# Reordering the first stage of a fused language-model tower: squares before tables, a weight's centring on ScalarE, rows worked ahead in two engines

## The chip, the cores and the metric

The kernel runs on one core of one Trainium2 chip. The metric is the device time of one execution in microseconds (us). The engines are named as the profile names them: PE is TensorE (PEld its weight loads), DVE is VectorE, ACT is ScalarE, POOL is GpSimd, SP is SyncE, which here only issues DMAs.

## The reference

The model takes 32 sequences of 128 tokens, with a vocabulary of 28, and has three parts. Cut to what matters here:

```python
h = tok(x, mask)                              # embedding + windowed features, fused @ fus_w, LayerNorm
h = h + attn(layernorm(h), Wq, Wk, Wv, Wo)    # 16 heads of 64, softmax, then LayerNorm(x + ctx @ Wo)
h = h + moe(layernorm(h))                     # 16 experts of 64, top 2, top 64 tokens of each expert
```

Before attention every token is a combination of 56 table rows (28 one-hot columns and 28 averages over neighbours), plus two constant rows. So each token's first LayerNorm needs only a quadratic form of its 56 coefficients, and the query, key, value and output weights can be multiplied with the 64-row table once, instead of with 4096 tokens. The last LayerNorm of attention subtracts a mean over 256 features; the kernel takes that mean out of the rows of Wo beforehand ("centring of the output weight").

## The kernel before

It is one program in three blocks, and at the end of each block all engines meet before the next one starts. The first block (lines 212 to 638) makes the tables; the second (751 to 1214) runs attention over 32 sequences; the third (1283 to 1538) runs the experts. Only the first block is touched. Each engine runs its own instruction list strictly in the order written, with semaphore waits between them; nobody plans or reorders. The core of the first block, after the table of 64 rows (`mt`) is there, is:

- **quads(g)**, for four octets g of sequences. PE L580 multiplies the transposed coefficients `nT` with a Gram matrix `cs` held in three bf16 parts (24 matmuls in two banks, `QUAD_BANKS[g % 2]`); DVE L423 multiplies the result with the coefficients `nb` (two instructions), and DVE L427 sums it into `red`. PE may refill a pair of banks only when DVE has read them (`prod_ok`).
- **roots**, DVE L445 to L455 with two square roots on ACT (L300): `r1`, `r2`, `r12`, `sig` for all 32 sequences, in a chain of small instructions. After the second root ACT loads the table for Exp (L301).
- **u_rows(g)**: DVE L460 and L461 scale the coefficients into `uf`; ACT L305 rounds them to f16 (`uh`, named u_hi); DVE L463 takes the remainder (`ul`).
- **u_cols(g)**: PE L597 transposes `uh` and `ul` of an octet into four banks, `UT_BANKS` (16 matmuls); ACT L309 copies each bank to `ub`. For the next octet PE waits for the copies of the one before, bank by bank (`ut_ok`).
- **table(n)**, n = 0, 1, 2 for Wq, Wk, Wv: PE L566 makes 16 fp32 products with `mt` (32 instructions in the trace), DVE L413 copies the bank to `qkv_t`, DVE L415 adds the bias column. Table 2 uses the bank of table 0 and waits for its copy.
- **centre_wo**: DVE L481, L483, L485 sum the rows of Wo (`wo_v`, 128x8x256), scale the sums and add them back in place.
- **gram**: PE L605 multiplies tables 0 and 1 head by head; ACT L314 (g_hi) and then DVE L468 (g_lo) store it as two f16 parts `gp`.
- **z_part(n)**, four of them: PE L619 multiplies table 2 with Wo in fp32; ACT L320 (z_hi) and then DVE L475 (z_lo) store it as `zh` and `zl`.
- **keep_going(n)**: n matmuls (L506) whose result nobody reads.

The lists of the three engines from there on, before the change: PE table(0), quads(0) to (3) with eight fillers ahead of (2) and of (3), table(1), table(2), eight fillers, u_cols(0), gram, then eight fillers and u_cols(g) for g = 1, 2, 3, and z_part(0) to (3). DVE centre_wo, table(0), four quads, roots, u_rows(0), table(1), u_rows(1), table(2), g_lo, u_rows(2), u_rows(3), four z_lo; each u_rows there has the remainder L463 in it. ACT stands in lines 298 to 337. POOL splits the expert weight w1 meanwhile (L268 to L272). SP issues its loads early, ahead of all this, in an order that isn't touched; Wo is the last of the four large weights (L235).

Of the kernel before, what the change touches and what calls it, by code (L numbers as in the profile page):

```python
# [89 lines left out]
def build(nc, d, out):  # L90
    with ExitStack() as ctx:
# [40 lines left out]
        def sb1(name, shape, dt=F32):  # L132
            return sb(name, shape, dt, one)
# [26 lines left out]
        wsum = sb1("wsum", [P, 2, HD])  # L160
# [22 lines left out]
        uf_ok, uh_ok, ul_ok, ut_ready, ut_ok = (sem(n) for n in ("uf_ok", "uh_ok", "ul_ok", "ut_ready", "ut_ok"))  # L183
# [28 lines left out]
        with nc.Block() as block:  # L212
# [66 lines left out]
            def _(act):  # L279
# [18 lines left out]
                for n, (v, root) in enumerate(((v1, q1), (v2, q2))):  # L298
                    act.wait_ge(v_ok, n + 1)
                    nc.scalar.activation(root[:], v[:], ACT.Sqrt).then_inc(sqrt_ok, 1)  # L300
                nc.scalar.preload_act_table(ACT.Exp)  # L301

# [22 lines left out]
                for n in range(4):  # L325
                    u_cols(0, n)
                g_hi()
                u_hi(2)
                for n in range(4):
                    u_cols(1, n)  # L330
                u_hi(3)
                for n in range(4):
                    u_cols(2, n)
                for n in range(4):
                    u_cols(3, n)
                for n in range(4):
                    z_hi(n)

            @block.vector
            def _(dve):  # L340
# [69 lines left out]
                def table(n):  # L410
                    dve.wait_ge(in_w[n], 32)
                    dve.wait_ge(qkv_ready, n + 1)
                    nc.vector.tensor_copy(qkv_t[:, n], TABLE_BANKS[n][:].rearrange("p (c u) -> p c u", c=HD)).then_inc(qkv_ok, 1)  # L413
                    dve.wait_ge(qkv_ok, 2 * n + 1)
                    nc.vector.tensor_copy(qkv_t[:, n, :, ONE:ONE + 1], bT[:, n, :].rearrange("p (c o) -> p c o", o=1))\  # L415
                        .then_inc(qkv_ok, 1)

# [38 lines left out]

                def u_rows(g):
# [3 lines left out]
                    nc.vector.tensor_copy(uf[:, s, R2:R2 + 1], r2[:, s].rearrange("p (b o) -> p b o", o=1)).then_inc(uf_ok, 1)  # L461
                    dve.wait_ge(uh_ok, g + 1)
# [16 lines left out]
                def centre_wo():  # L479
                    dve.wait_ge(in_wo, 16)  # L480
                    nc.vector.reduce_sum(wsum[:, 0, :], wo_v, AX.X).then_inc(wo_step, 1)  # L481
                    dve.wait_ge(wo_step, 1)
                    nc.vector.tensor_scalar(wsum[:, 1, :], wsum[:, 0, :], -1.0 / D, None, ALU.mult).then_inc(wo_step, 1)  # L483
                    dve.wait_ge(wo_step, 2)
                    nc.vector.tensor_tensor(wo_v, wo_v, bcast(wsum[:, 1, :], D), ALU.add).then_inc(wo_step, 1)  # L485

                centre_wo()
                table(0)
# [4 lines left out]
                table(1)  # L493
                u_rows(1)
                table(2)
                g_lo()
                u_rows(2)
                u_rows(3)
# [4 lines left out]
            def _(pe):  # L503
# [81 lines left out]
                def u_cols(g):  # L585
# [5 lines left out]
                    for n in range(4):  # L591
                        if g >= 1:
                            pe.wait_ge(ut_ok, 4 * g - 3 + n)
# [16 lines left out]
                def z_part(n):  # L610
                    if n == 0:
                        pe.wait_ge(wo_step, 3)
                        pe.wait_ge(qkv_ok, 6)
                        pe.wait_ge(glo_ok, len(G_PARTS))
# [8 lines left out]

                table(0)
                for g in range(NQ):
                    if g >= 2:
                        keep_going(8, psum[0][:, 0:FREE])
                    quads(g)
# [5 lines left out]
                for g in range(1, NQ):  # L634
                    keep_going(8, psum[5][:, 0:FREE])
                    u_cols(g)
# [958 lines left out]
```

## Time and profile before

| | |
|---|---|
| median of 3 runs | 570.81 us (569.54 to 571.08) |
| the profiled execution | 572.44 us, of which the span from first to last instruction is 570.7 us |
| first block | 0 to 66.8 us of the span |
| busy PE, DVE, ACT, POOL over the whole span | 526.0, 453.3, 357.1, 387.5 us |
| mean granted clock of PE | 0.963 of full speed |

How to read it: the page's busy shares are means over three blocks. PE is 92% busy over the whole span, which is set by the two later blocks. What matters here is the first block, and in it which engine each other engine waits for. The strip of the whole span in 40 slices of 14.3 us shows it: PE is granted its full clock nearly everywhere except in slices 3 to 5.

```
PE   4797788999999999999999999839999999999985
DVE  5785466889888888888888888977846888887776
ACT  1215767788787877878878787614784655565540
PEclk9957799999999999999999999987999999999998
```

### The profile page before, as it was taken

What the parts mean: (1) busy time and instruction counts of PE and PEld (TensorE: products, weight loads), DVE (VectorE), ACT (ScalarE), POOL (GpSimd) and SP (SyncE); (2) the same over time, 40 slices, a digit from 0 to 9 for tenths busy, and PEclk for the clock granted to TensorE, in tenths of its full rate; (3) what the DMA queues carried; (4) which work ended last, traced back from release to release, by engine and by line L of the source; (5) the groups of instructions that cost most, each with busy time, mean ns of one, the idle gap of its engine ahead of it and who ended that gap; (6) DMA issues with size and microseconds to landing.
All of it is one profiled execution on the core that took longest, in us unless ns stands there. A gap on an engine that the chain in (4) does not pass through costs nothing. (4 is left out here: it accounts for less than half of the span.)

```text
span 570.7 us, 16170 instructions
## 1 busy us (share of the span) xinstructions
PE 526.0 (92%) x6063; PEld 395.0 (69%) x6063; DVE 453.3 (79%) x1019; ACT 357.1 (63%) x744; POOL 387.5 (68%) x512
## 2 busy tenths in 40 slices
PE   4797788999999999999999999839999999999985
PEld 2697666778777777777777777624457777777774
DVE  5785466889888888888888888977846888887776
ACT  1215767788787877878778787614584655565540
POOL 3050235888787877878778787942095977898783
PEclk9957799999999999999999999987999999999998
DMA  6800000000000000000000000000633044053011
GB/s 208 325 2 1 2 1 2 4 3 2 3 3 3 2 3 3 3 3 3 4 3 2 4 3 3 2 0 2 151 85 83 20 110 102 22 141 85 24 45 55
DMA packets 11905, 21.73 MB, mean 38 GB/s; under 512 B 4668, under 2 KB 9780, under 8 KB 10164
## 3 DMA queue, kind: packets, MB, share of 16 engines
q1 hardware_dynamic: 11828, 20.71, 13.1%
q8 instruction: 48, 0.79, 0.6%
q14 instruction: 29, 0.24, 0.1%
HBM read 16.24 MB, written 4.33 MB: 36 GB/s over the span
## 5 line engine op out<-in xcount | busy, mean ns | idle before, releaser
L768 POOL TENSOR_TENSOR s_pl<-s_pf,s_ph 128x512 f16<-128x512 f32 x128 | 147.0, 1160 | 15.3 <-ACT s_ph L860 15.3
L949 DVE TENSOR_REDUCE s_mx<-ps 128x4 f32<-128x512 f32 x128 | 83.8, 677 | 29.1 <-PE ps L1090 29.1
L1503 PE MATMUL ps<-s_xt_all,s_w1s 128*128 128x512 f16 x384 | 89.9, 387 | 0.8 <-PEq L751 0.8
L1526 PE MATMUL ps<-s_w2s,s_hid 128*128 128x256 f16 x768 | 88.9, 273 | 0.0
L854 ACT ACTIVATE s_pf<-ps 128x512 f32<-128x512 f32 x128 | 76.6, 602 | 16.9 <-PE ps L1103 16.9
L1526 PEld LDWEIGHTS ps<-s_w2s,s_hid 128*128 128x128 f16 x768 | 75.1, 98 | 11.1
L860 ACT ACTIVATE s_ph<-s_pf 128x512 f16<-128x512 f32 x128 | 77.2, 637 | 0.0
L1136 PE MATMUL ps<-s_zh,s_cth 128*128 128x256 f16 x256 | 69.8, 273 | 0.0
L1136 PE MATMUL ps<-s_zl,s_cth 128*128 128x256 f16 x256 | 69.8, 273 | 0.0
L1136 PE MATMUL ps<-s_zh,s_ctl 128*128 128x256 f16 x256 | 69.8, 273 | 0.0
L1503 PEld LDWEIGHTS ps<-s_xt_all,s_w1s 128*128 128x128 f16 x384 | 38.1, 100 | 42.4 <-issue 4.5
L1120 PE MATMUL ps<-s_uh,s_ph 128*128 128x64 f16 x512 | 51.5, 193 | 0.4 <-issue 0.4
L1120 PE MATMUL ps<-s_ul,s_ph 128*128 128x64 f16 x512 | 51.5, 193 | 0.0
L1120 PE MATMUL ps<-s_uh,s_pl 128*128 128x64 f16 x512 | 51.5, 193 | 0.0
L1341 POOL TENSOR_TENSOR s_hid<-s_ub,s_hid 128x512 f16<-128x512 f32 x24 | 29.8, 1264 | 29.3 <-ACT s_hid L1382 29.1
L1103 PE MATMUL ps<-s_qh,s_ub 64*128 64x512 f16 x256 | 48.9, 379 | 0.0
L847 ACT ACTIVATE s_qh<-ps 128x512 f16<-128x512 f32 x64 | 38.1, 596 | 16.3 <-PE ps L1103 14.3
L940 DVE SCALAR_TENSOR_TENSOR s_ql<-ps,s_qh 128x512 f16<-128x512 f32 x64 | 43.3, 678 | 5.2 <-ACT s_qh L847 5.2
L1120 PEld LDWEIGHTS ps<-s_uh,s_ph 128*128 128x128 f16 x512 | 46.1, 98 | 1.1 <-issue 0.6
L1120 PEld LDWEIGHTS ps<-s_ul,s_ph 128*128 128x128 f16 x512 | 45.4, 98 | 0.7
L1120 PEld LDWEIGHTS ps<-s_uh,s_pl 128*128 128x128 f16 x512 | 45.5, 98 | 0.0
L970 DVE TENSOR_TENSOR s_ctl<-ps,s_cth 128x512 f16<-128x512 f32 x64 | 43.6, 682 | 0.4 <-ACT s_cth L866 0.3
(230 smaller groups left out, 1252.3 us busy)
## 6 DMA issues: line engine op xcount, KB each, us to landing
s_rep<-picks SPq DMA_DIRECT2D x14, 512.0 KB, 6.6
s_stage<-in_w SPq DMA_DIRECT2D x2, 1024.0 KB, 13.9
out<-s_ot_a SPq DMA_DIRECT2D x16, 128.0 KB, 1.7
out<-s_lg SPq DMA_DIRECT2D x16, 128.0 KB, 1.7
s_stage<-in_wq SPq DMA_DIRECT2D x1, 1024.0 KB, 4.7
s_stage<-in_wk SPq DMA_DIRECT2D x1, 1024.0 KB, 6.4
s_stage<-in_wv SPq DMA_DIRECT2D x1, 1024.0 KB, 8.1
s_stage<-in_wo SPq DMA_DIRECT2D x1, 1024.0 KB, 9.9
```

The lines of the kernel that those rows point to most:

```text
L768: nc.gpsimd.tensor_tensor(flat(pl[:, b % 2, 4 * j:4 * j + 4, :]), pf[:, j, :], flat(ph[:, b % 2, 4 * j:4 * j + 4, :]), ALU.subtract).then_ ...
L847: nc.scalar.activation(flat(qh[:, b % 2, hf]), A[hf][:], ACT.Copy, scale=1.0 / G_SCALE)\
L854: nc.scalar.activation(pf[:, j, :], ST[j % 2][:], ACT.Exp).then_inc(exp_done[j], 1)
L860: nc.scalar.activation(flat(ph[:, b % 2, 4 * j:4 * j + 4, :]), pf[:, j, :], ACT.Copy).then_inc(phi_done[j], 1)
L940: nc.vector.scalar_tensor_tensor(out=flat(ql[:, b % 2, hf]), in0=A[hf][:], scalar=1.0 / G_SCALE, in1=flat(qh[:, b % 2, hf]), op0=ALU.mult, ...
L949: nc.vector.tensor_reduce(mx[:, b % 2, c:c + 4], A[ab][:].rearrange("p (h k) -> p h k", h=4), AX.X, ALU.max).then_inc(max_done[hf][ab], 1)
L970: nc.vector.tensor_tensor(flat(ctl[:, b % 2, 4 * hf:4 * hf + 4, :]), CB[hf][:], flat(cth[:, b % 2, 4 * hf:4 * hf + 4, :]), ALU.subtract).t ...
L1103: mm = nc.tensor.matmul(ST[ab][:], ub[r, b, part, :], flat(q[r, b % 2, hf]), start=(n == 0), stop=(n == 2))
L1120: mm = nc.tensor.matmul(CB[hf][:, c:c + UD], p[:, b % 2, h, :], u[:, b, 0, :], start=(n == 0), stop=(n == 2))
L1136: nc.tensor.matmul(YB[:, 0:D], c[:, b % 2, p, :], zz[:, p, :], start=(p == 0 and c is cth and zz is zh), stop=False)
L1503: mm = nc.tensor.matmul(HB[j % NH][:], w1s[:, wp, c, j * P:(j + 1) * P], xt_all[:, GB * g:GB * (g + 1), xp, c, :], start=(k == 0), stop=(k ...
L1526: mm = nc.tensor.matmul(zb[b % 4], hid[:, g % 2, hp, j, t * P:(t + 1) * P], w2s[:, wp, j, :], start=False, stop=(j == NJ - 1 and hp == 1))
```

## The change

Within the first block, with no work added to or taken from the result:

- PE issues twelve fillers, quads(0), quads(1), then table(0), then quads(2), quads(3), table(1), table(2). The fillers ahead of quads(2) and (3) are gone; those ahead of the later u_cols are six instead of eight.
- Centring of the output weight moves from DVE (three instructions) to ACT: eight sums of 256 columns by an Identity with an accumulator, each waiting for the one before, one scaling, and eight in-place additions (Identity with a bias per partition).
- The copies of the three tables and of their bias columns move from DVE to ACT, placed between the centring steps and the square roots.
- DVE starts with the quads. Its u_rows is split in scaling (`u_rows`) and remainder (`u_lo`), and scaling is issued one octet ahead. ACT's u_hi(2) comes ahead of the copies of octet 0, and u_hi(3) ahead of g_hi.
- The fourth bank of each octet's u_cols is copied by DVE instead of ACT, with a semaphore of its own (`ut_last_ok`). ACT's copies of octet 3 go between z_hi(1) and z_hi(2).

```diff
--- before.py
+++ after.py
@@ -157,7 +157,7 @@
         mt = sb1("mt", [P, 2, KC, 2, UD])
         cs, cres = sb1("cs", [P, 3, P], BF16), sb1("cres", [P, P])
         s_eps = sb1("s_eps", [P, 1])
-        wsum = sb1("wsum", [P, 2, HD])
+        wsum, wo_sum = sb1("wsum", [P, 2, HD]), sb1("wo_sum", [P, D])
         prod = tok[:, 0:B // 2, :].rearrange("p n (k a u) -> p (n k) a u", k=2, a=2)
         red = sb1("red", [P, B, 2])
         v1, r1, t1, q1, t2, t3, v2, r2, r12, q2 = (
@@ -180,7 +180,7 @@
         quad_ready, prod_ok, red_ok = sem("quad_ready"), sem("prod_ok"), sem("red_ok")
         root_step, v_ok, sqrt_ok = sem("root_step"), sem("v_ok"), sem("sqrt_ok")
         root_count = [0]
-        uf_ok, uh_ok, ul_ok, ut_ready, ut_ok = (sem(n) for n in ("uf_ok", "uh_ok", "ul_ok", "ut_ready", "ut_ok"))
+        uf_ok, uh_ok, ul_ok, ut_ready, ut_ok, ut_last_ok = (sem(n) for n in ("uf_ok", "uh_ok", "ul_ok", "ut_ready", "ut_ok", "ut_last_ok"))
         qkv_ready, qkv_ok, g_ready, ghi_ok, glo_ok, z_ready, zhi_ok, zlo_ok, wo_step = (
             sem(n) for n in ("qkv_ready", "qkv_ok", "g_ready", "ghi_ok", "glo_ok", "z_ready", "zhi_ok", "zlo_ok", "wo_step"))
 
@@ -295,10 +295,32 @@
                 nc.scalar.activation(tts[0:UD, :], tm[:], ACT.Copy, scale=T_SCALE).then_inc(tts_ok, 1)
                 nc.scalar.activation(mr[0:UD, :], mbo[:], ACT.Copy, scale=Y_SCALE).then_inc(mr_ok, 1)
 
-                for n, (v, root) in enumerate(((v1, q1), (v2, q2))):
+                def root(n, v, r):
                     act.wait_ge(v_ok, n + 1)
-                    nc.scalar.activation(root[:], v[:], ACT.Sqrt).then_inc(sqrt_ok, 1)
+                    nc.scalar.activation(r[:], v[:], ACT.Sqrt).then_inc(sqrt_ok, 1)
+
+                def table(n):
+                    act.wait_ge(in_w[n], 32)
+                    act.wait_ge(qkv_ready, n + 1)
+                    nc.scalar.activation(qkv_t[:, n], TABLE_BANKS[n][:].rearrange("p (c u) -> p c u", c=HD), ACT.Copy).then_inc(qkv_ok, 1)
+                    act.wait_ge(qkv_ok, 2 * n + 1)
+                    nc.scalar.activation(qkv_t[:, n, :, ONE:ONE + 1], bT[:, n, :].rearrange("p (c o) -> p c o", o=1), ACT.Copy)\
+                        .then_inc(qkv_ok, 1)
+
+                act.wait_ge(in_wo, 16)
+                for c in range(HD):
+                    nc.scalar.activation(wo_sum[:], wo_v[:, c, :], ACT.Identity, accum_out=wsum[:, 0, c:c + 1]).then_inc(wo_step, 1)
+                    act.wait_ge(wo_step, c + 1)
+                nc.scalar.activation(wsum[:, 1, :], wsum[:, 0, :], ACT.Copy, scale=-1.0 / D).then_inc(wo_step, 1)
+                act.wait_ge(wo_step, HD + 1)
+                table(0)
+                for c in range(HD):
+                    nc.scalar.activation(wo_v[:, c, :], wo_v[:, c, :], ACT.Identity, bias=wsum[:, 1, c:c + 1]).then_inc(wo_step, 1)
+                root(0, v1, q1)
+                table(1)
+                root(1, v2, q2)
                 nc.scalar.preload_act_table(ACT.Exp)
+                table(2)
 
                 def u_hi(g):
                     act.wait_ge(uf_ok, 2 * g + 2)
@@ -322,19 +344,20 @@
 
                 u_hi(0)
                 u_hi(1)
-                for n in range(4):
+                u_hi(2)
+                for n in range(3):
                     u_cols(0, n)
+                u_hi(3)
                 g_hi()
-                u_hi(2)
-                for n in range(4):
-                    u_cols(1, n)
-                u_hi(3)
-                for n in range(4):
-                    u_cols(2, n)
-                for n in range(4):
+                for g in (1, 2):
+                    for n in range(3):
+                        u_cols(g, n)
+                z_hi(0)
+                z_hi(1)
+                for n in range(3):
                     u_cols(3, n)
-                for n in range(4):
-                    z_hi(n)
+                z_hi(2)
+                z_hi(3)
 
             @block.vector
             def _(dve):
@@ -407,14 +430,6 @@
                 nc.vector.scalar_tensor_tensor(out=mr[UD:P, :], in0=mbo[:], scalar=Y_SCALE, in1=mr[0:UD, :],
                                                op0=ALU.mult, op1=ALU.subtract).then_inc(mr_ok, 1)
 
-                def table(n):
-                    dve.wait_ge(in_w[n], 32)
-                    dve.wait_ge(qkv_ready, n + 1)
-                    nc.vector.tensor_copy(qkv_t[:, n], TABLE_BANKS[n][:].rearrange("p (c u) -> p c u", c=HD)).then_inc(qkv_ok, 1)
-                    dve.wait_ge(qkv_ok, 2 * n + 1)
-                    nc.vector.tensor_copy(qkv_t[:, n, :, ONE:ONE + 1], bT[:, n, :].rearrange("p (c o) -> p c o", o=1))\
-                        .then_inc(qkv_ok, 1)
-
                 def quads(g):
                     for par in range(2):
                         dve.wait_ge(quad_ready, 2 * g + par + 1)
@@ -454,11 +469,19 @@
                     then(nc.vector.tensor_tensor(r12[:], r1[:], r2[:], ALU.mult))
                     then(nc.vector.scalar_tensor_tensor(out=sig[:], in0=v2[:], scalar=1.0 / T_SCALE, in1=r2[:], op0=ALU.mult, op1=ALU.mult))
 
+                def u_cols(g):
+                    dve.wait_ge(ut_ready, 4 * g + 4)
+                    nc.vector.tensor_copy(ub_b[:, 4 * g + 3, :], UT_BANKS[3][:]).then_inc(ut_last_ok, 1)
+
                 def u_rows(g):
                     s = octet(g)
                     dve.wait_ge(cleared, CLEARED["uf"])
                     nc.vector.tensor_tensor(uf[:, s, 0:2 * V], nb[:, s, 0:2 * V], bcast(r12[:, s], 2 * V), ALU.mult).then_inc(uf_ok, 1)
                     nc.vector.tensor_copy(uf[:, s, R2:R2 + 1], r2[:, s].rearrange("p (b o) -> p b o", o=1)).then_inc(uf_ok, 1)
+
+                def u_lo(g):
+                    s = octet(g)
+                    dve.wait_ge(uf_ok, 2 * g + 2)
                     dve.wait_ge(uh_ok, g + 1)
                     nc.vector.tensor_tensor(ul[:, s], twice(uf[:, s, :]), uh[:, s], ALU.subtract).then_inc(ul_ok, 1)
 
@@ -476,26 +499,21 @@
                                                    scalar=Y_SCALE, in1=zh[:, zc, :], op0=ALU.mult, op1=ALU.subtract)\
                         .then_inc(zlo_ok, 1)
 
-                def centre_wo():
-                    dve.wait_ge(in_wo, 16)
-                    nc.vector.reduce_sum(wsum[:, 0, :], wo_v, AX.X).then_inc(wo_step, 1)
-                    dve.wait_ge(wo_step, 1)
-                    nc.vector.tensor_scalar(wsum[:, 1, :], wsum[:, 0, :], -1.0 / D, None, ALU.mult).then_inc(wo_step, 1)
-                    dve.wait_ge(wo_step, 2)
-                    nc.vector.tensor_tensor(wo_v, wo_v, bcast(wsum[:, 1, :], D), ALU.add).then_inc(wo_step, 1)
-
-                centre_wo()
-                table(0)
                 for g in range(NQ):
                     quads(g)
                 roots()
                 u_rows(0)
-                table(1)
                 u_rows(1)
-                table(2)
+                u_lo(0)
+                u_rows(2)
+                u_lo(1)
+                u_cols(0)
+                u_rows(3)
+                u_lo(2)
                 g_lo()
-                u_rows(2)
-                u_rows(3)
+                u_lo(3)
+                for g in range(1, NQ):
+                    u_cols(g)
                 for n in range(4):
                     z_lo(n)
 
@@ -589,8 +607,10 @@
                     if g == 0:
                         pe.wait_ge(prod_ok, 2 * NQ)
                     for n in range(4):
-                        if g >= 1:
-                            pe.wait_ge(ut_ok, 4 * g - 3 + n)
+                        if g >= 1 and n < 3:
+                            pe.wait_ge(ut_ok, 3 * g - 2 + n)
+                        elif g >= 1:
+                            pe.wait_ge(ut_last_ok, g)
                         for k in range(2):
                             for a, src in ((0, uh), (1, ul)):
                                 x = (2 * k + a) * P
@@ -609,7 +629,7 @@
 
                 def z_part(n):
                     if n == 0:
-                        pe.wait_ge(wo_step, 3)
+                        pe.wait_ge(wo_step, 2 * HD + 1)
                         pe.wait_ge(qkv_ok, 6)
                         pe.wait_ge(glo_ok, len(G_PARTS))
                     for m, p in enumerate(Z_CHUNKS[n]):
@@ -621,18 +641,19 @@
                                                   start=True, stop=True)
                     mm.then_inc(z_ready, 1)
 
+                keep_going(12, psum[0][:, 0:FREE])
+                quads(0)
+                quads(1)
                 table(0)
-                for g in range(NQ):
-                    if g >= 2:
-                        keep_going(8, psum[0][:, 0:FREE])
-                    quads(g)
+                quads(2)
+                quads(3)
                 table(1)
                 table(2)
                 keep_going(8, psum[0][:, 0:FREE])
                 u_cols(0)
                 gram()
                 for g in range(1, NQ):
-                    keep_going(8, psum[5][:, 0:FREE])
+                    keep_going(6, psum[5][:, 0:FREE])
                     u_cols(g)
                 for n in range(4):
                     z_part(n)
```


## Rows read from the trace of the kernel before

**Rows 1.** Stretch, length, busy PE, PEld, DVE, ACT, POOL (instructions), granted clock, DMA
```profile
27.30:36.70 9.40, 7.51 (x76) 6.88 (x77) 9.23 (x14) 0.00 (x0) 7.95 (x6) 0.66 0.02 4
```

**Rows 2.** Timeline of VectorE up to its square roots: start, duration, instruction, idle before
```profile
20.66 0.29 DVE L402 TENSOR_TENSOR s_cs<-s_cres,s_cs 128x128 bf16<-128x128 f32 x1 [0.31 <-ACT s_cs L293]
...
21.77 2.29 DVE L481 TENSOR_REDUCE s_wsum<-s_stage 128x8 f32<-128x2048 f32 x1
...
26.50 0.68 DVE L413 COPY s_qkv_t<-ps 128x512 f32<-128x512 f32 x1
...
27.30 1.29 DVE L423 TENSOR_TENSOR s_h<-ps,s_nb 128x512 f32<-128x512 f32 x2
...
36.70 0.62 DVE L445 TENSOR_SCALAR s_v<-s_red 128x32 f32<-128x32 f32 x1
```

**Rows 3.** Timeline of TensorE in the first stage and at the next one's start
```profile
19.51 3.76 PE L566 MATMUL ps<-s_mt,s_stage 128*128 128x64 f32 x32
23.21 1.51 PE L580 MATMUL ps<-s_cs,s_nT 64*128 64x128 bf16 x48
24.65 0.97 PE L506 MATMUL ps<-s_masked,s_ident 128*128 128x232 bf16 x8
...
32.45 13.91 PE L566 MATMUL ps<-s_mt,s_stage 128*128 128x64 f32 x64
...
61.95 2.01 PE L619 MATMUL ps<-s_stage,s_qkv_t 64*64 64x256 f32 x32
66.77 1.05 PE L1077 MATMUL ps<-s_ub,s_gp 128*128 128x128 f16 x16 [2.82 <-PEq L212]
```

**Rows 4.** TensorE in single microseconds: length, busy time, granted clock (1.00 is full)
```profile
23.00:24.00 1.00, 1.00 (x32) 1.00 1.09 451
30.00:31.00 1.00, 0.60 (x5) 0.62 0.00 0
```

**Rows 5.** The 16 matmuls of L597 for one octet, at either clock
```profile
51.95:52.84 0.89, 0.89 (x16) 1.00 0.00 0
57.74:59.41 1.67, 1.67 (x16) 0.50 0.00 0
```

**Rows 6.** Timeline of ScalarE in the first stage
```profile
20.84 0.40 ACT L296 ACTIVATE s_mr<-s_mbo 64x256 f16<-64x256 f32 x1
37.35 0.23 ACT L300 ACTIVATE s_q<-s_v 128x32 f32<-128x32 f32 x1 [16.11 <-DVE s_v L445]
...
40.59 1.28 ACT L301 ACT_TABLE_LOAD   x1
43.15 1.06 ACT L305 ACTIVATE s_uh<-s_uf 128x1024 f16<-128x1024 f32 x1 [1.27 <-DVE s_uf L461]
...
51.28 1.41 ACT L314 ACTIVATE s_gp<-ps 64x128 f16<-64x128 f32 x8 [0.85 <-PE ps L605]
...
63.31 2.10 ACT L320 ACTIVATE s_zh<-ps 128x512 f16<-128x512 f32 x4
```

**Rows 7.** ScalarE by line and shape: busy us, mean ns
```profile
L1388 ACT ACTIVATE s_zl<-s_h,s_nmr,s_rx_all 128x256 f32<-128x256 f32 x32 | 18.8, 589 | 7.3 <-DVE ps L1440 7.2
...
L893 ACT ACTIVATE s_ysq<-ps 128x256 f32<-128x256 f32 x32 | 12.3, 384 | 31.1 <-PE ps L1141 31.1
...
L893 ACT ACTIVATION_READ_ACCUMULATOR s_ysq<-ps 128x1 f32 x32 | 6.2, 194 | 0.0
```

**Rows 8.** Timeline of VectorE in the rest of the first stage
```profile
44.24 1.23 DVE L463 TENSOR_TENSOR s_ul<-s_uf,s_uh 128x1024 f16<-128x1024 f32 x1 [1.12 <-ACT s_uh L305]
...
46.18 0.62 DVE L460 TENSOR_TENSOR s_uf<-s_nb,s_r 128x448 f32<-128x448 bf16 x1
46.71 0.17 DVE L461 COPY s_uf<-s_r 128x8 f32<-128x8 f32 x1
...
52.73 1.67 DVE L468 SCALAR_TENSOR_TENSOR s_gp<-ps,s_gp 64x128 f16<-64x128 f32 x8 [2.69 <-ACT s_gp L314]
...
63.97 2.48 DVE L475 SCALAR_TENSOR_TENSOR s_zl<-ps,s_zh 128x512 f16<-128x512 f32 x4 [3.51 <-ACT s_zh L320]
```

## Prediction

> **What bounds the kernel now.** The blocks meet at their ends, so I read only the first one, by engine. First the stretch by engine in which DVE works on the quads [rows 1]: DVE is busy 9.23 of 9.40 us, ACT 0.00, PE at a mean clock of 0.66. Then DVE's timeline [rows 2]: it is free of the preparations at 21.77, and up to 27.30 it does the centring (21.77 to 26.50, 4.73 us) and the copy of table 0 with its bias (0.80 us), while the first quads wait. From 27.30 the four quads run back to back to 36.70, the roots follow, and ACT, idle for 16.11 us before its first root [rows 6], starts the first u_hi at 43.15. Next PE's timeline [rows 3]: table 0, the first 48 quad matmuls and eight fillers, then a hole until DVE frees a bank. After that the clock falls: 1.00 at 23 to 24 us, 0.62 (a mean of both levels, 2.4 and 1.2 GHz) at 30 to 31 [rows 4]. Tables 1 and 2 then take 13.91 us for 64 instructions, 217 ns each, where table 0 took 3.76 for 32, 117 each [rows 3]. They end at 46.36, about one u_lo behind the first ul, which is done at 45.47 [rows 8]. Last the tail: DVE waits for ACT in each row (1.12, 2.69 and 3.51 us) [rows 8] and ACT for DVE [rows 6]. The last z_lo ends at 63.97 + 2.48 = 66.45, and the next block's first matmul is at 66.77 [rows 3, 8]. So the bound is a chain that goes through DVE, then PE at 1.2 GHz, then DVE and ACT by turns.
>
> **Squares first.** PE has its last operand when L402 ends, 20.95 [rows 2]. The twelve fillers take 12/8 of 0.97 = 1.46 us from about 19.5 and end at about the same moment. 24 quad matmuls are 1.51/2 = 0.75 us [rows 3]: the first are ready at 21.8, as DVE comes free. The 48 end at 22.5. Table 0 takes 3.7 (start to start, 19.51 to 23.21), until 26.2, then quads(2) until 27.0. DVE has finished two quads at 21.8 + 2 x 2.33 = 26.45, so it waits 0.55 us. The four end at 21.8 + 9.40 + 0.55 = 31.75 in place of 36.70: **4.95 us earlier**. If table 0 ran at 1.2 GHz, 3.2 us of this would be lost.
>
> **Centring and table copies on ACT.** ACT is free at 20.84 + 0.40 = 21.24 [rows 6], and Wo has landed by 21.77, as L481 reads it. A sum with accumulator on 128x256: L893 takes 384 + 194 ns [rows 7], from PSUM and with some overlap; the trace has none from SBUF, so between 0.45 (overlapped) and 0.8 us (L1388's 589 plus 194); I take 0.55, near L893. Eight: 4.4 (3.6 to 6.4). Scaling: 0.2. Table copy: like one of L320, 0.6, bias column 0.2. Eight additions with a bias per partition: between 0.38 and 0.59 each [rows 7]; I take 0.45 as one follows the other without a wait: 3.6 (3.0 to 4.7). Table 0 is ready at 26.2; ACT comes to it at 21.24 + 4.4 + 0.2 = 25.9. Then 26.2 + 0.8 + 3.6 = 30.6. The first root is wanted at 31.75 + 0.65 = 32.4: hidden, with 1.8 us to spare; at the upper ends (33.2) it would cost 0.8. What waits behind these instructions in ACT's list is that root, and behind it DVE's whole root chain.
> [...]
>
> **Tables 1 and 2.** PE starts table 1 after quads(3) at 27.7. PE has been busy without a hole since before 19.51, and table 0 of the same kind left the clock at 1.00 [rows 4]; so 3.7 each: 31.4 and 35.2 in place of 46.36. ACT copies table 1 after the first root, done by 33.5. The second root was wanted at 40.3, just ahead of the Exp load at 40.59 [rows 6], now at 35.4. Exp load 1.28: until 36.9, table 2 copied until 37.8. The first u_hi, 43.15 - 4.95 = **38.2**, isn't held up. ACT is 0.4 us ahead. If these tables ran at 1.2 GHz, they would end at 27.7 + 13.9 = 41.6 and u_hi(0) would start at 42.45.
>
> **The rows worked ahead.** From here both engines are the chain. Prices: scaling 0.7 (L460 and L461), u_lo 1.23, g_lo 1.67 [rows 8], u_hi 1.06, g_hi 1.41, z_hi 2.10/4 start to start [rows 6], DVE's bank copy 0.68 like L413 [rows 2], ACT's about 0.5 like z_hi, 16 transposes 0.89 at 2.4 GHz and 1.67 at 1.2 [rows 5]. ACT: u_hi(0) 38.2 to 39.25, u_hi(1) to 40.25. DVE: rows(1) to 38.9, u_lo(0) 39.3 to 40.5, rows(2) 41.15, u_lo(1) 42.4. PE ends its fillers at 36.2 and idles 4.4 us until u_lo(0); a hole of that kind was followed by the low clock before, so I cost u_cols(0) at 1.67: 40.6 to 42.4, gram until 44.1. DVE's copy of the fourth bank 43.2, rows(3) 43.85. ACT: u_hi(2) 42.2, three copies 43.7, u_hi(3) 43.9 to 44.95, g_hi 46.3. DVE: u_lo(2) 45.1, g_lo 46.3 to 48.0, u_lo(3) 49.1, copy for octet 1 49.7. ACT's copies of octet 1 end at 47.8. PE's u_cols(1) is long done; u_cols(2) waits in its fourth bank for 49.7 and ends at 50.0. Six fillers 0.7, u_cols(3) 0.9: 51.6. z_part 2.01 [rows 3]: 53.6, its first quarter at 52.1. ACT: z_hi(0), (1) until 53.3, three copies until 54.8, z_hi(2), (3) until 55.85. DVE: the last z_lo (2.48/4, at its full length 0.7) ends at **56.6**, against 66.45. From u_hi(0) to the end it was 23.3 us and is 18.4.
> New waits here: in DVE g_lo stands 1.2 us for g_hi with u_lo(3) queued behind it, and PE's third octet waits for that; in ACT two z_hi stand ahead of the copies of octet 3, which nobody but the next block needs. Unknown is the clock in 47 to 54 us, when PE has holes again. At 1.2 GHz the last transposes and the z products would take 2.2 us more; at 2.4 from 40.6 on, the sum would not change, since ACT and DVE set it.
>
> **Sum.** Removed from the block: 66.45 - 56.6 = 9.85 us: 4.95 ahead of the first u_hi and 4.9 behind. Nothing in the later blocks is changed, SP's loads are issued as before and POOL's split has its data as before. At the start of the next block PE was idle for 2.82 us before [rows 3], now about 3.4: much the same clock; half a low stretch more or less is up to 1 us. Span 570.7 - 9.85 = 560.85, profiled time 572.44 - 9.85 = 562.6. The median of the runs is 1.63 below the profiled one: 570.81 - 9.8 = **561.0 us**.
>
> **Rivals.**
> (1) The clock falls in the long run of fp32 tables. For: they ran 13.91 us at 1.2 GHz without bringing it back, so they may count for little. Against: it stayed up after table 0. Then u_hi(0) is 42.45 and all behind is 4.25 late: 565.2 us. If it falls already in table 0, quads(2) is 3.2 late, table 2 ends near 45.7, and u_hi(0) starts at 46.5: 569.3, which measures as the same.
> (2) ACT becomes the bound: sums and additions at their upper ends or above. At 0.8 and 0.59 it costs 0.8; at 1 us each, 21.24 + 16 + 1 = 38.2, root 5.8 late: 566.8. It decides from about 0.7 us a piece. For: the eight sums wait for each other. Against: all ACT rows of 256 columns lie below 0.6.
> (3) Low clock at the end of the block, during z: 563.2.
> (4) Slower. The clock doesn't come back after the boundary, since it now comes after a longer hole. Each us at 1.2 GHz costs PE, which is filled there, half of one. The gain is gone when it lasts 20 us longer, which tables 1 and 2 show to be possible; at 30 us more it is 576. Against: the block opens with dense f16 matmuls and fillers, as it did before.
> (5) The reordering doesn't take place in effect: DVE still waits for PE at its first quads. The operands are there at 20.95, so only if the fillers ran at 1.2 GHz (1.4 us more): 562.4.
>
> **Chances.** Forecast with (5) 0.57, (3) 0.15, (1) at 565 0.11, (1) at 569 0.03, (2) 0.08, (4) 0.03, a gain over 11.3 us 0.03. The forecast alone spans 559.5 to 562.5. The range reaches to (1) and (3): 559.5 to 565.8. A measurement of this kernel tells 0.3% (1.7 us) from no change. Faster by more than that 0.94, within it 0.03, slower 0.03.
>
> **What would show it.** In the changed profile: quads on DVE from 21.8 with one gap near 26.5; the ACT centring done by 31; L566 at 117 ns throughout; first u_hi near 38.2; last z_lo near 56.6 and the next block 0.3 later, with everything behind shifted by the same. The forecast is wrong if PE's clock reads 0.50 between 27 and 35 us, if DVE waits for ACT at its first reciprocal for more than 1 us, or if the second block is longer than before.

## The result and the profile after

| | before | after |
|---|---|---|
| median | 570.81 us (569.28 to 571.33, 5 runs) | 567.74 us (565.99 to 568.68, 5 runs) |
| ratio | | 0.9943 (0.9925 to 0.9961) |
| profiled execution, its span | 572.44, 570.7 us | 568.68, 566.9 us |
| busy PE, DVE, ACT, POOL | 526.0, 453.3, 357.1, 387.5 us | 517.8, 453.1, 364.3, 385.9 us |
| mean granted clock | 0.963 | 0.975 |

The change gains 3.07 us by the medians, 3.76 between the two profiled executions; 9.85 was forecast. The profiled execution of the kernel before, with a mean clock of 0.963, is a rare one: of its 41 executions timed beside the experiments three read 0.963 to 0.966 (572.2 to 572.5 us), the others 0.972 to 0.981 (568.6 to 572.2 us). The five of the changed kernel read 0.972 to 0.978.

The page's strip of the whole span shows where PE's clock rose most, in slice 3 (5 before, 9 after); slices 4 and 5, with the rest of the first block and the boundary, read 7 in both:

```profile
PE   4957789999999999999999999739999999999985
PEclk9997799999999999999999999988999999999999
```

Four moments of the profiled executions say where the gain went. K is the second group of eight matmuls with `qh` in the second block (L1090 before, L1111 after). From K to the end of the span it is 496.6 us before and 497.0 after: nothing that matters lies behind it. The forecast of K is that of the block plus the 7.35 us which it took before.

| | before | forecast | after | gained |
|---|---|---|---|---|
| v1, first step of the roots | 36.70 | 31.75 | 31.61 | 5.09 |
| first u_hi | 43.15 | 38.2 | 42.00 | 1.15 |
| next block's first matmul | 66.77 | 56.9 | 61.47 | 5.30 |
| K | 74.12 | 64.3 | 69.92 | 4.20 |

**The first half is as forecast.** VectorE's timeline after, to be read against [rows 2]:

```profile
21.68 1.29 DVE L438 TENSOR_TENSOR s_h<-ps,s_nb 128x512 f32<-128x512 f32 x2 [0.18 <-PE ps L598]
...
26.86 1.29 DVE L438 TENSOR_TENSOR s_h<-ps,s_nb 128x512 f32<-128x512 f32 x2 [0.45 <-PE ps L598]
...
31.61 1.74 DVE L460 TENSOR_SCALAR s_v<-s_red 128x32 f32<-128x32 f32 x1
33.72 0.35 DVE L451 RECIPROCAL s_r<-s_q 128x32 f32<-128x32 f32 x1 [0.37 <-ACT s_q L300]
34.11 3.41 DVE L452 TENSOR_TENSOR s_t<-s_v,s_r 128x32 f32<-128x32 f32 x1
37.55 0.19 DVE L453 TENSOR_TENSOR s_t<-s_t,s_r 128x32 f32<-128x32 f32 x1
```

**The roots are not.** Two of their small instructions have grown. L460 takes 1.74 us, in place of 0.62 [rows 2], and L452 takes 3.41 where its neighbour of the same shape takes 0.19. Neither waits for a semaphore: the time is inside the instruction, so the view of waits doesn't list it. GpSimd's timeline after, and the same three instructions before:

```profile
31.42 1.90 POOL L270 TENSOR_SCALAR s_stage<-s_stage 128x2048 f32<-128x2048 f32 x1
33.41 4.06 POOL L272 TENSOR_TENSOR s_w1s<-s_stage,s_w1s 128x2048 f16<-128x2048 f32 x1
```

```profile
29.24 1.90 POOL L268 TENSOR_SCALAR s_w1s<-s_stage 128x2048 f16<-128x2048 f32 x1
31.22 1.90 POOL L270 TENSOR_SCALAR s_stage<-s_stage 128x2048 f32<-128x2048 f32 x1
33.20 4.08 POOL L272 TENSOR_TENSOR s_w1s<-s_stage,s_w1s 128x2048 f16<-128x2048 f32 x1
```

L460 ends at 33.35, POOL's L270 at 33.32; L452 ends at 37.52, POOL's L272 at 37.47. Before, L445 ended at 37.32 and L272 at 37.28. POOL didn't move, VectorE's chain moved 5 us forward, into it.

ScalarE after, to be read against [rows 6]: the eight sums are 0.54 apart (0.55 forecast), the eight additions 0.41 apart (0.45), all done at 30.2 and hidden.

```profile
21.43 0.42 ACT L312 ACTIVATE s_wo_sum<-s_stage 128x256 f32<-128x256 f32 x1
21.75 0.18 ACT L312 ACTIVATION_READ_ACCUMULATOR s_wo_sum<-s_stage 128x1 f32 x1
21.97 0.42 ACT L312 ACTIVATE s_wo_sum<-s_stage 128x256 f32<-128x256 f32 x1
...
26.91 3.29 ACT L318 ACTIVATE s_stage<-s_stage,s_wsum 128x256 f32<-128x256 f32 x8
33.39 0.23 ACT L300 ACTIVATE s_q<-s_v 128x32 f32<-128x32 f32 x1 [3.19 <-DVE s_v L460]
```

TensorE after, to be read against [rows 3]: tables 1 and 2 take 7.36 us for 64 instructions, at the full clock. The next block opens with 1.87 us for the sixteen that took 1.05.

```profile
27.42 7.36 PE L584 MATMUL ps<-s_mt,s_stage 128*128 128x64 f32 x64
...
61.47 1.87 PE L1098 MATMUL ps<-s_ub,s_gp 128*128 128x128 f16 x16 [3.81 <-PEq L212]
```

PE in single microseconds (length, busy PE, PEld, DVE, ACT, POOL, granted clock, DMA), after and then before: the clock falls in the idle 3.8 us ahead of the block and comes back at 67 to 68. Before it fell when the block had begun and was back at 71 to 72.

```profile
60.00:61.00 1.00, 0.00 (x0) 0.00 (x0) 1.00 (x2) 0.32 (x1) 0.00 (x0) 0.69 0.00 0
66.00:67.00 1.00, 1.00 (x7) 0.76 (x6) 0.82 (x2) 0.00 (x0) 0.83 (x3) 0.50 0.00 0
67.00:68.00 1.00, 1.00 (x14) 0.64 (x13) 0.00 (x0) 0.00 (x0) 1.00 (x1) 0.89 0.00 0
```

```profile
67.00:68.00 1.00, 1.00 (x18) 0.92 (x16) 0.00 (x0) 0.58 (x2) 1.00 (x1) 0.89 0.16 24
70.00:71.00 1.00, 1.00 (x7) 0.72 (x6) 0.66 (x2) 0.33 (x1) 1.00 (x1) 0.50 0.00 0
71.00:72.00 1.00, 1.00 (x15) 0.71 (x13) 0.22 (x1) 0.00 (x0) 0.92 (x2) 0.90 0.00 0
```

### The profile page after: what moved, and what is told of

It reads as the page before. It is cut to its first block and busy times, and to the rows that moved or that the text cites. A ratio compares the mean times of both kernels' runs of the same rounds, so it can differ in the third digit from the quotient of the medians.

```text
span 566.9 us, 16176 instructions
## 1 busy us (share of the span) xinstructions
PE 517.8 (91%) x6053; PEld 386.9 (68%) x6053; DVE 453.1 (80%) x1014; ACT 364.3 (64%) x771; POOL 385.9 (68%) x512
## 5 line engine op out<-in xcount | busy, mean ns | idle before, releaser
L1362 POOL TENSOR_TENSOR s_hid<-s_ub,s_hid 128x512 f16<-128x512 f32 x24 | 29.7, 1257 | 30.7 <-ACT s_hid L1403 30.2
L868 ACT ACTIVATE s_qh<-ps 128x512 f16<-128x512 f32 x64 | 38.2, 596 | 16.9 <-PE ps L1124 14.4
L1141 PEld LDWEIGHTS ps<-s_uh,s_ph 128*128 128x128 f16 x512 | 46.1, 98 | 1.1 <-issue 0.6
```

Of the source, the lines that this page charges most:

```text
L1141: mm = nc.tensor.matmul(CB[hf][:, c:c + UD], p[:, b % 2, h, :], u[:, b, 0, :], start=(n == 0), stop=(n == 2))
L1362: nc.gpsimd.tensor_tensor(hid[:, g % 2, 1, j, :], gelu_tile(g, j), hid[:, g % 2, 0, j, :], ALU.subtract)\
```

## The experiments

**The theory**: VectorE's roots are held inside their instructions while a GpSimd instruction runs on SBUF, and PE's clock at the block's boundary takes part of what is left. **The rival for the first loss**: the roots became longer by themselves (ScalarE's new work between its two roots, or the new order), so moving GpSimd's work changes nothing. **The rival for the rest**: the clock doesn't matter there, and the worked-ahead rows bring less than forecast.

All in one table, moments in us of each profiled execution. K to the end of the span is 496.1 to 497.3 in all of them, so the last moment carries the total. Each row of moments is one execution. The kernels were timed in three groups, in which the kernel before had medians of 570.80, 571.10 and 570.45, so across groups a difference of medians is good to about half a microsecond, and the ratios are the safer measure. In late_dummy_write and late_tables_first the preparations end 2.0 us later than in after_split_late (the eight matmuls of `mt` ahead of the fillers start at 19.88 and 19.90, there at 17.86), ahead of any edit; this much of their moments belongs to no edit.

| kernel | v1 | first u_hi | next block | K | span | median (range, runs) | ratio to before |
|---|---|---|---|---|---|---|---|
| before | 36.70 | 43.15 | 66.77 | 74.12 | 570.7 | 570.81 (569.28–571.33, 5) | 1 |
| after | 31.61 | 42.00 | 61.47 | 69.92 | 566.9 | 567.74 (565.99–568.68, 5) | 0.9943 (0.9925–0.9961) |
| after_split_late | 31.57 | 37.17 | 58.25 | 66.54 | 563.0 | 564.92 (561.54–566.57, 4) | 0.9886 (0.9839–0.9933) |
| before_split_late | 36.38 | 42.40 | 66.14 | 73.49 | 569.8 | 570.21 (567.67–572.06, 10) | 0.9984 (0.9965–1.0004) |
| late_dummy_read | 31.67 | 40.98 | 62.07 | 70.28 | 566.6 | 568.42 (1 run) | |
| late_dummy_write | 33.59 | 40.29 | 59.77 | 68.14 | 564.6 | 566.37 (1 run) | |
| after_fill_end | 31.21 | 41.59 | 61.08 | 66.76 | 562.9 | 565.79 (564.84–566.43, 4) | 0.9902 (0.9884–0.9920) |
| late_fill_both | 32.05 | 37.65 | 59.20 | 64.89 | 562.2 | 563.38 (562.59–563.95, 4) | 0.9860 (0.9843–0.9878) |
| late_tail_old | 31.51 | 37.12 | 58.98 | 66.33 | 562.8 | 565.28 (564.09–566.22, 4) | 0.9893 (0.9871–0.9915) |
| late_centre_dve | 36.54 | 42.56 | 66.04 | 73.38 | 570.4 | 572.01 (570.41–574.17, 10) | 1.0022 (1.0002–1.0041) |
| late_tables_first | 35.22 | 44.30 | 63.77 | 71.89 | 568.2 | 567.90 (563.70–570.38, 10) | 0.9950 (0.9920–0.9980) |
| late_fill_all | 31.52 | 37.12 | 56.14 | 61.83 | 558.9 | 561.24 (560.73–561.87, 4) | 0.9834 (0.9811–0.9856) |
| late_copy_early | 32.18 | 37.78 | 55.90 | 61.58 | 558.7 | 560.47 (559.59–562.64, 5) | 0.9828 (0.9800–0.9856) |

### GpSimd's split out of the way

after_split_late is the changed kernel, before_split_late the kernel before, each with POOL's split of `w1` moved from the first block to the second, behind its split of `w2`:

```diff
-                split(both(w1s[:, 0]), both(w1s[:, 1]), stage2[:, 0, :], 3)
@@ second block, behind pool.wait_ge(w_hi, 7)
+                nc.gpsimd.tensor_scalar(both(w1s[:, 0]), stage2[:, 0, :], W_SCALE, 0.0, ALU.mult, ALU.add).then_inc(w_split, 1)
...
```

> The changed kernel, but GpSimd's split of the expert weight w1 (8 us in three instructions) is issued in the second block, behind the split of w2, instead of beside VectorE's root chain. Theory A (the roots lose their time because a VectorE instruction with two SBUF inputs, or one in its fast mode, can't run beside a GpSimd instruction that reads SBUF): L460 falls from 1.74 to about 0.25 us and the first L452 from 3.41 to 0.19, the first u_hi starts near 37.3 instead of 42.0, the block ends 4.7 us earlier, and the time is near 563 us. Theory B (the two long instructions have another cause, such as a fetch of code or the loads): they stay long and the time stays at 567.7. Theory C (the split is needed where it was, since the second block's start has no room on GpSimd): the first block is shorter but the time is 566 or more.

> The kernel before, with the same move of GpSimd's split. Theory A: in this kernel the split ends as the roots begin, so only L445 (0.62 to 0.25 us) and the wait before the first reciprocal (0.78 us) shrink: 0.4 to 0.9 us, 570 us. Theory B: no change, 570.8. If it gains 4 us as the changed kernel should, the split costs something else than the roots.

VectorE's timeline of after_split_late:

```profile
31.57 0.18 DVE L459 TENSOR_SCALAR s_v<-s_red 128x32 f32<-128x32 f32 x1
32.11 0.35 DVE L450 RECIPROCAL s_r<-s_q 128x32 f32<-128x32 f32 x1 [0.37 <-ACT s_q L299]
32.50 0.19 DVE L451 TENSOR_TENSOR s_t<-s_v,s_r 128x32 f32<-128x32 f32 x1
```

1.74 us has become 0.18 and 3.41 has become 0.19. The first u_hi starts 4.83 us earlier than in the changed kernel, with ScalarE's work and order untouched, so the rival for the first loss falls. In the kernel before, the same move brings the first u_hi 0.75 us forward, of which 0.32 lie ahead of v1, and by the medians nothing that can be told: the conflict cost there its 0.44 us in L445. It is the change that made it dear. Behind u_hi some of the gain goes again: the block starts 3.22 us earlier, not 4.83, and the median, 564.92, is 1.9 above the 563 expected. The clock falls once more in the tail, and z runs at the low level: 2.89 us, where the changed kernel and [rows 3] have 2.01.

```profile
50.00:51.00 1.00, 1.00 (x14) 1.00 (x12) 0.16 (x1) 0.00 (x0) 0.00 (x0) 0.51 0.00 0
```

```profile
51.54 2.89 PE L638 MATMUL ps<-s_stage,s_qkv_t 64*64 64x256 f32 x32
```

In its second block POOL's moved split runs from 68.65 to 76.68, and the first instruction behind it starts at 79.06 after 2.38 us idle. K to the end is 496.5 us, so the move costs nothing that can be seen there.

before_split_late shows something else besides. Its list on PE ahead of tables 1 and 2 is that of the kernel before, and so is the hole of 3.12 us in it, but here the tables ran at the full clock from 33 us on and ended 6.5 us earlier:

```profile
32.13 7.72 PE L565 MATMUL ps<-s_mt,s_stage 128*128 128x64 f32 x64
```

The block started only 0.63 us earlier, less than the 0.75 that the first u_hi brought with it: the faster products gained the block nothing here, in part because z ran at the low clock, 3.63 us. What decided the clock behind that hole stays open.

### Which instruction is held by which

Both kernels are after_split_late with something for POOL to do once `v1` is done. The results are overwritten later by the real split, so nothing of the computation changes. Each was run once. late_dummy_read has an instruction that reads SBUF, late_dummy_write two that only write it:

```diff
+                pool.wait_ge(v_ok, 1)
+                nc.gpsimd.tensor_tensor(both(w1s[:, 1]), stage2[:, 0, :], stage2[:, 1, :], ALU.subtract)
```

```diff
+                pool.wait_ge(v_ok, 1)
+                nc.gpsimd.memset(both(w1s[:, 1]), 0.0)
+                nc.gpsimd.memset(both(w1s[:, 0]), 0.0)
```

> after_split_late with one more GpSimd instruction whose result is overwritten later: a subtraction of two 128x2048 SBUF tensors (about 4 us), started when the first variance v1 is ready. Theory A: the first VectorE instruction with two SBUF inputs after the reciprocal (L452) takes 3 to 4 us again and the first u_hi is that much later, at 41. Theory B: L452 stays at 0.19 us.

> after_split_late with two GpSimd memsets of 128x2048 f16 each (1 to 2 us each) at the same place: GpSimd is busy, writes SBUF, but reads nothing. Theory A in the form that only reads collide: L452 stays at 0.19 us and the first u_hi at 37.3; in the form that any GpSimd work collides: L452 takes as long as the memsets last, 2 to 4 us.

late_dummy_read, GpSimd and VectorE:

```profile
31.93 4.51 POOL L277 TENSOR_TENSOR s_w1s<-s_stage 128x2048 f16<-128x2048 f32 x1 [2.83 <-DVE s_v L461]
```

```profile
32.22 0.35 DVE L452 RECIPROCAL s_r<-s_q 128x32 f32<-128x32 f32 x1 [0.36 <-ACT s_q L301]
32.60 3.89 DVE L453 TENSOR_TENSOR s_t<-s_v,s_r 128x32 f32<-128x32 f32 x1
36.52 0.19 DVE L454 TENSOR_TENSOR s_t<-s_t,s_r 128x32 f32<-128x32 f32 x1
```

late_dummy_write, GpSimd and VectorE:

```profile
33.83 1.80 POOL L277 MEMSET s_w1s<- 128x2048 f16 x1 [5.17 <-DVE s_v L462]
35.57 1.84 POOL L278 MEMSET s_w1s<- 128x2048 f16 x1
```

```profile
34.52 0.19 DVE L454 TENSOR_TENSOR s_t<-s_v,s_r 128x32 f32<-128x32 f32 x1
34.75 0.19 DVE L455 TENSOR_TENSOR s_t<-s_t,s_r 128x32 f32<-128x32 f32 x1
34.98 0.69 DVE L456 TENSOR_SCALAR s_t<-s_t 128x32 f32<-128x32 f32 x1
...
36.62 0.82 DVE L468 TENSOR_SCALAR s_v<-s_t,s_s_eps 128x32 f32<-128x32 f32 x1
```

The stall comes back with POOL's reading instruction: the two-input instruction ends at 36.49, POOL's at 36.44, and v1 to u_hi takes 9.31 us, against 5.60 in after_split_late and 6.70 beside the memsets. Against a writer alone, two-input instructions keep their 0.19 us, but the one-input TENSOR_SCALARs end with the memsets (35.67 and 35.63, 37.44 and 37.41). RECIPROCAL keeps its 0.35 beside the reader and beside the writer. The quads, which take one of their two operands from PSUM, aren't held either: in [rows 1] POOL is busy for 7.95 of 9.40 us, and the quads take the 1.29 us of [rows 2] there as they do at 21.68 after, with POOL idle beside them.
This is what the Trainium skill states (page "SBUF — State Buffer", section "Who interferes with whom"): VectorE and GpSimd share one pair of ports as an exclusive lock; an instruction with two SBUF inputs contends with a GpSimd instruction that reads SBUF, one in a 2-port mode with any, and whoever is first holds it for its whole length. The trace agrees: the six pairs of ends given here and under the profile after lie within 0.05 us of each other. That GpSimd in its turn can be held by VectorE, no run here shows.

### The clock at the boundary

after_fill_end is the changed kernel with 34 fillers behind the last z product, so that PE isn't idle when the blocks meet; late_fill_both has these, GpSimd's split moved, and 44 fillers in place of 8 ahead of the first u_cols.

```diff
                 for n in range(4):
                     z_part(n)
+                pe.wait_ge(ut_last_ok, NQ)
+                keep_going(34, psum[7][:, 0:FREE])
```

> The changed kernel with 34 fillers more on TensorE behind the last z product, which keep it busy until the block's end (3.3 us at full clock) and write a bank that nobody reads any more. Theory A (1.1 us of the gain are lost because the hole of 3.8 us at the boundary leaves TensorE at 1.2 GHz for the first 5.6 us of the second block): the granted clock stays 1.00 from 57 us on, and the matmuls that took 8.45 us from the block's start to the second group of L1090 take 5 to 7; the time falls by 1 to 2.8 us to 565 to 566.7. Theory B (the start of the second block is set by VectorE and ScalarE): the clock is up, but the time stays within 0.5 us of 567.7.

> after_split_late with 44 instead of 8 fillers ahead of the first u_cols, so that the hole of 4.3 us is filled, and 34 fillers behind the last z product. Theory A (what is missing to the 561.0 us forecast, 3.9 us, is TensorE's clock in z and over the boundary): z takes 2.0 instead of 2.9 us, the second block starts at full clock, and the time is 561 to 562.5 us. Theory B (ScalarE and VectorE set both places): 564 to 565 with the clock at 1.00 throughout.

after_fill_end, TensorE: the block opens at the full clock.

```profile
57.20 3.54 PE L524 MATMUL ps<-s_masked,s_ident 128*128 128x232 bf16 x34
61.08 1.05 PE L1100 MATMUL ps<-s_ub,s_gp 128*128 128x128 f16 x16 [0.33 <-PEq L212]
```

From the block's start to K it takes 5.68 us, in the changed kernel 8.45 and before 7.35. So the low clock cost 2.8 us there after and 1.7 before, and the change lost 1.1 by it. The longer hole comes with the new tail: it is 3.81 us in every kernel that has it and no fillers, 2.82 before and 2.83 in late_tail_old. Its length alone doesn't decide the cost: late_centre_dve has 3.81 too, opens the block at the full clock, loses it at 67 to 68 as the kernel before does, and takes 7.34 us to K.

```profile
66.04 1.05 PE L1103 MATMUL ps<-s_ub,s_gp 128*128 128x128 f16 x16 [3.81 <-PEq L212]
```

The median is 1.95 us below the changed kernel's (2.3 by the ratios); of the 4.0 us between the profiled spans, 0.4 lie ahead of v1 and 0.8 behind K, and belong to no edit. late_fill_both keeps the boundary (5.69) but not z (2.98 us at the low clock): PE still had holes at 44.5 to 46.1, where it waited for ScalarE's bank copies, and at 47.3 to 49.0, for VectorE's copy of the fourth bank of octet 1. Its 563.38 lies above the 561 to 562.5 expected, as z stayed slow.

### The three parts of the change, each undone

GpSimd's split is moved in all three, so that it doesn't blur them. late_tail_old has the order of before from the first u_hi on, and ScalarE copies all banks; late_centre_dve has centring and table copies on VectorE, as before; late_tables_first has PE's order of before:

```diff
-                keep_going(12, psum[0][:, 0:FREE])
+                table(0)
                 quads(0)
                 quads(1)
-                table(0)
                 quads(2)
```

> after_split_late with the order of the kernel before from the first u_hi on: rows not worked ahead, all bank copies on ScalarE, z_hi last. Theory A (the rows worked ahead are worth what the forecast put down for them, 4.9 us less what the faster tables give): 3 to 5 us slower than after_split_late, 568 to 570. Theory B (that part of the gain came from tables 1 and 2 at full clock, and the order hardly matters): within 1 us of 564.9.

> after_split_late with the centring and the three table copies back on VectorE, centring and table 0 ahead of the first quads, tables 1 and 2 between the rows. Theory A (the move to ScalarE is worth what it takes from VectorE's list: 4.73 + 0.80 less the 0.45 us that quads(2) waits, and two more copies in the tail): 5 to 6.5 us slower, 570 to 571.5. Theory B (ScalarE has become as late as VectorE): 2 us slower or less.

> after_split_late with TensorE's order of the kernel before at the start: table(0) ahead of quads(0) and (1), without the twelve fillers. Theory A (squares first is worth what the first quads wait for table 0): VectorE's first quads start near 24 instead of 21.6 us, but quads(2) no longer waits 0.45 us, so the roots start 2 us later and the time is 566.5 to 567.5. Theory B (VectorE's being free of the centring is all that counts, and TensorE catches up): within 0.7 us of 564.9.

**The tail** is worth 0.7 us at the block's start (58.98 against 58.25) and nothing at K, where the old order is even 0.2 ahead (66.33 against 66.54), since it crosses the boundary with the shorter hole; the medians, 565.28 and 564.92, are the same. Its gain depends on PE: with z at the full clock in both, u_hi to block is 21.86 us in the old order and 19.47 in the changed kernel, 2.4 us; but after_split_late pays 1.6 of this back at the low clock. The other 1.8 us of what looked like the tail (23.62 before, 21.86 here) came with the order of before unchanged, from the tables: their copies had stood in VectorE's list behind its first u_rows, and their products at the low clock in PE's. before_split_late, with fast products and the copies still on VectorE, parts the two in part: from u_hi to z it takes 17.86 us, against 18.80 before and 17.03 in late_tail_old. But its z then ran at the low clock, 3.63 us, and u_hi to block is 23.74, no shorter than before.

**Centring and table copies on ScalarE** carry the change: without them 572.01, 7.1 us more than after_split_late (5 to 6.5 were expected; by the ratios it is 7.8), and 0.2% slower than the kernel before. v1 is back at 36.54 and tables 1 and 2 at 1.2 GHz:

```profile
32.30 13.91 PE L584 MATMUL ps<-s_mt,s_stage 128*128 128x64 f32 x64
```

**Squares ahead of the tables**: 3.0 us by the medians (3.7 by the ratios; 1.6 to 2.6 were expected). The profiled execution has the quads at 25.83 in place of 21.63, 2.0 of which is its late start, holes before quads(2) and (3), then the tables at the low clock, and u_hi behind the last of them on ScalarE:

```profile
25.83 1.29 DVE L437 TENSOR_TENSOR s_h<-ps,s_nb 128x512 f32<-128x512 f32 x2 [2.35 <-PE ps L597]
```

```profile
27.27 0.85 PE L597 MATMUL ps<-s_cs,s_nT 64*128 64x128 bf16 x24 [0.80 <-DVE s_h L437]
29.58 0.85 PE L597 MATMUL ps<-s_cs,s_nT 64*128 64x128 bf16 x24 [1.47 <-DVE s_h L437]
30.36 13.10 PE L583 MATMUL ps<-s_mt,s_stage 128*128 128x64 f32 x64
```

```profile
43.56 0.60 ACT L304 ACTIVATE s_qkv_t<-ps 128x512 f32<-128x512 f32 x1 [4.01 <-PE ps L583]
```

The ten runs spread from 563.70 to 570.38, and their mean clocks with them (0.980 to 0.983 in the three at 563.70 to 564.27, 0.963 in the five from 568.19 up). That the short ones kept the full clock in the tables fits this, but none of them was profiled. So the 3.0 us is a mean over two behaviours, and the profiled execution shows the longer one.

### Both losses removed

late_fill_all is late_fill_both with twelve more fillers ahead of octet 2 and sixteen between its third and fourth bank. late_copy_early takes the wait away instead: VectorE copies the fourth bank of octet 1 ahead of g_lo, and twelve and ten more fillers stand ahead of octets 2 and 3.

```diff
                 u_lo(2)
+                u_cols(1)
                 g_lo()
                 u_lo(3)
-                for g in range(1, NQ):
+                for g in range(2, NQ):
@@ PE
-                    keep_going(6, psum[5][:, 0:FREE])
+                    keep_going((6, 18, 16)[g - 1], psum[5][:, 0:FREE])
```

> late_fill_both with 12 fillers more ahead of the third octet's transposes and 16 between its third and fourth bank, where TensorE stood for 1.5 and 1.9 us and the clock fell just ahead of z. Theory A (z and the last transposes run at 1.2 GHz because of these holes, and cost 1.9 us): the clock stays 1.00 from 40 us on, z takes 2.0 us, and the time is 561 to 562 us. Theory B (the end of the block is set by ScalarE and VectorE): z is faster but the block ends where it did, 563.4.

> late_fill_both with VectorE's copy of octet 1's fourth bank moved ahead of g_lo, where VectorE is idle for 1.3 us, and 12 and 10 fillers more ahead of the third and fourth octets. Theory A (the forecast's tail missed that this copy, behind g_lo and u_lo(3), holds TensorE's third octet and with it z): z starts 1 to 1.5 us earlier than in late_fill_both besides running at full clock, the block ends near 56.5, and the time is 560 to 561.5 us, the fastest of all. Theory B: u_lo(3) is as late as the copy was, and the time equals that of late_fill_all.

late_copy_early, TensorE:

```profile
50.09 2.01 PE L639 MATMUL ps<-s_stage,s_qkv_t 64*64 64x256 f32 x32
52.03 3.54 PE L524 MATMUL ps<-s_masked,s_ident 128*128 128x232 bf16 x34
55.90 1.05 PE L1105 MATMUL ps<-s_ub,s_gp 128*128 128x128 f16 x16 [0.33 <-PEq L212]
```

In both, z takes 2.01 us and the block's start to K 5.7. u_hi to block is 19.0 and 18.1 us; the forecast had 18.4 to the last z_lo and 18.7 to the block. late_fill_all measures 561.24, where the change alone was forecast at 561.0. The early copy moves the block 0.9 us nearer to u_hi, but the medians (561.24 and 560.47) can't be told apart. late_copy_early is the fastest kernel here: 10.0 us below the kernel before that ran beside it (570.45), 7 below the changed one.

## Why the prediction was wrong

- **Squares first: right.** DVE starts at 21.68 (forecast 21.8), one gap of 0.45 (0.55), v1 at 31.61 (31.75).
- **Centring and tables on ScalarE: right**, by size and as hidden. Rivals (1), (2) and (5) didn't come, and (4) only in small, as the 1.1 us below. Without the part the kernel is 7.1 us slower.
- **Tables 1 and 2: right**, 7.36 us against 7.4 forecast. The reading that PE at 1.2 GHz was a link of the old chain isn't borne out: before_split_late had the products in 7.72 us and its block only 0.63 us earlier, though its slow z blurs this.
- **First u_hi at 38.2: wrong by 3.8 us**, and this is the step that failed. I took the way from v1 to u_hi over as a fixed 6.45 us, and costed POOL's unmoved split at nothing ("POOL's split has its data as before"). It took 10.39 us: 1.56 and 3.22 us of holding, of which 0.44 was in the old time already. Free of POOL it is 5.60; the old 6.45 held 0.44 of POOL and 0.41 of a longer wait for the first root (0.78 us, 0.37 after), which the kernels have in which ScalarE was idle for some 16 us ahead of that root (before_split_late 0.77, late_centre_dve 0.78). No rival named this; the row was there: [rows 1] shows POOL busy 7.95 of 9.40 us in the stretch into which the roots were moved, and L445 [rows 2] takes 0.62 us, where TENSOR_SCALARs of its shape take 0.18.
- **Worked-ahead rows: 4.9 forecast, 4.14 measured** (23.30 to 19.16, to the end of the last z_lo), 0.3 us of the miss on PE up to z, the rest in ScalarE's copies and z_hi. The attribution was wrong besides: 1.8 of it belongs to the tables, and 2.4 to the order, while z is at the full clock. With the boundary's longer hole, which comes with the new tail, 1.1 of the 2.4 go again.
- **The boundary, "much the same clock": wrong by 1.1 us.** The hole is 3.81, not 3.4, and the low stretch costs 2.8 us, not 1.7.
- **Behind K**: 0.4 us, within what the kernels differ there.

In sum 3.8 + 0.76 + 1.1 + 0.4 = 6.06 us of the 6.09 that are missing (9.85 less 3.76) between the profiled executions. In the medians 6.74 are missing: the forecast took the median to be 1.63 below the profiled time as before, and after it is 0.94 below. Rival (3), the low clock in z, is wrong for the changed kernel (2.01) and came in after_split_late (2.89), but it doesn't hang on the stall alone: late_dummy_read has the stall and z at 2.77. Of the three signs of being wrong that the prediction named, two didn't show, and the third, a longer second block, stood only for the 1.1 us: none of them looked at the roots. That it would be faster by over 0.3% was right, the range was not: it bounded each moved part by the clock and by the engine that does it, and by nothing that runs beside it.

## What to carry to other kernels

When a chain is moved in time, list what each other engine does in the stretch it moves to. A small VectorE instruction with SBUF operands can take as long as the GpSimd instruction beside it, and shows this as its own duration, without any wait. And a shorter first stage with an emptier PE pays at the next dense stretch: fill the hole, or count the low clock there.

## What the runs showed of the hardware that I had not expected

- Small 128x32 VectorE instructions took 3.41 and 3.89 us in place of 0.19 beside a GpSimd TENSOR_TENSOR, and 0.69 and 0.82 in place of 0.18 and 0.24 beside memsets; in these traces only VectorE was seen held, and the 4.06 to 4.08 us of GpSimd's L272 didn't change.
- fp32 products of the tables kept the full clock for 7.36 us when PE came to them without a hole, and took 13.1 to 13.9 us, nearly all at 1.2 GHz, in three profiles in which it came after holes; in a fourth, before_split_late, with the same list ahead of them and the same hole as the kernel before, they took 7.72 us, at the full clock from 33 us on.
- 34 fillers in a hole of 3.8 us at a block's boundary took 2.8 us off the 8.45 us behind it.
